# Node sums ahead of the transposes in TensorE's order of the first layer

## What is computed

```python
h = relu(layernorm(x))                                # 12500 x 16
hidden = relu(edge_attr_16 @ W1 + b1)                 # 412500 x 256
w_edge = (hidden @ W2 + b2).reshape(-1, 16, 16)       # a 16x16 matrix for each edge
msgs   = einsum('ei,eio->eo', h[src], w_edge)         # 412500 x 16
aggr   = segment_sum(msgs, dst)                       # 12500 x 16
x      = x + relu(batchnorm(aggr + h @ root + bias))
```

## Time and profile before

| | before |
|---|---|
| median of three runs | 8360.46 us (8337.11 to 8364.19) |
| the profiled execution | 8371.47 us, span 8369.5 us |
| mean granted TensorE clock | 0.941 |
| TensorE matmul busy | 7304.6 us, 87% |
| VectorE busy | 6439.7 us, 77% |
| GpSimd busy | 5810.0 us, 69% |
| ScalarE busy | 4454.8 us, 53% |
| first layer, first to last gather | 59.4 to 5086.6 us |

### The profile page before, as it was taken

The page is one execution under the profiler, slowest core; times in us unless marked ns, Lnnn a source line. Parts: engine busy times, 40 slices in busy tenths (PEclk is TensorE's granted clock), DMA queues, the critical chain, the costliest instruction groups (busy, mean ns, idle before and its releaser), DMA issues. The chain is left out here.

```text
span 8369.5 us, 188597 instructions
## 1 busy us (share of the span) xinstructions
PE 7304.6 (87%) x52097; PEld 6359.6 (76%) x52097; DVE 6439.7 (77%) x16833; ACT 4454.8 (53%) x8278; POOL 5810.0 (69%) x4953
## 2 busy tenths in 40 slices
PE   6888887888888888888888886999999999999998
PEld 5666666666666666666666664999999999999996
DVE  6666666666666666666666667999999999999997
ACT  3333333333333333333333334777878777777874
POOL 5666666666666666666666664888888888888886
PEclk8999999999999999999999998999999999999999
DMA  2000001000000000000000004444444455554444
GB/s 50 16 16 16 16 16 16 16 16 16 16 16 16 16 16 16 16 16 16 16 16 16 16 16 96 75 73 73 74 73 75 73 72 73 73 72 74 74 73 65
DMA packets 702593, 335.08 MB, mean 40 GB/s; under 512 B 423055, under 2 KB 646234, under 8 KB 702562
## 3 DMA queue, kind: packets, MB, share of 16 engines
q0 software_dynamic: 336128, 66.50, 12.9%
q1 hardware_dynamic: 365248, 264.73, 12.9%
q10 hardware_dynamic: 1186, 3.51, 0.1%
HBM read 301.49 MB, written 32.76 MB: 40 GB/s over the span
## 5 line engine op out<-in xcount | busy, mean ns | idle before, releaser
L728 POOL DMA_INDIRECT xg<-gather_rows,idx x3232 | 3144.1, 973 | 1905.1 <-issue 1874.3
L838 PE MATMUL ps_w<-W2s,hT 128*128 128x256 f32 x12928 | 3351.9, 416 | 148.6 <-issue 137.8
L838 PEld LDWEIGHTS ps_w<-W2s,hT 128*128 128x128 f32 x12928 | 2726.1, 211 | 762.3 <-issue 250.7
L1590 POOL DMA_INDIRECT sums<-total,row x1616 | 2570.5, 1591 | 539.1 <-issue 437.5
L1553 PE MATMUL ps_wide<-hot_col,placed 128*128 128x392 f32 x12928 | 2434.1, 345 | 11.6 <-issue 5.1
L1553 PEld LDWEIGHTS ps_wide<-hot_col,placed 128*128 128x128 f32 x12928 | 2313.1, 195 | 38.8 <-issue 22.9
L767 ACT ACTIVATE hT<-ps_h,b1c 128x512 f32<-128x512 f32 x1616 | 1023.0, 681 | 2442.1 <-PE ps_h L826 1954.0
L899 DVE TENSOR_TENSOR prod<-ps_w,xg 128x512 f32<-128x512 f32 x1616 | 1097.7, 690 | 1285.0 <-remote 985.9
L1389 DVE SCALAR_TENSOR_TENSOR placed<-ps_r,src_r,halves 128x512 fp32r<-128x512 f32 x1616 | 1096.8, 740 | 0.1
L1488 ACT ACTIVATE square<-iota_col,minus_col 128x784 bf16<-128x784 int16 x1212 | 1059.1, 936 | 60.9 <-issue 52.1
L906 DVE TENSOR_REDUCE msg<-prod 128x32 f32<-128x512 f32 x1616 | 1058.8, 676 | 0.0
(11 more groups left out here) (203 smaller groups left out, 4680.8 us busy)
## 6 DMA issues: line engine op xcount, KB each, us to landing
dst_row<-dst_rows SPq DMA_DIRECT2D x404, 256.0 KB
xg<-gather_rows,idx POOLq DMA_INDIRECT x3232
src_row<-src_rows SPq DMA_DIRECT2D x404, 128.0 KB
q_win<-q_rows SPq DMA_DIRECT2D x404, 96.0 KB
ea<-in_edge_attr SPq DMA_DIRECT2D x404, 64.0 KB
sums<-total,row POOLq DMA_INDIRECT x1616
e<-in_edge_attr SPq DMA_DIRECT2D x404, 32.0 KB
q_rows<-Q SPq DMA_DIRECT2D x12, 768.0 KB, 5.4
```

The costliest lines, as they stand in the source:

```text
L728: pool.indirect_dma_start(xg[r][:, t, :], None, k.rows, bass.IndirectOffsetOnAxis(ap=idx[r][:, t:t + 1], axis=0)).then_inc(xg_in[r][t], 16)
L838: last = pe.matmul(bank[:, w, :, :].rearrange("p i o -> p (i o)"), hT[half][:, j, col:col + P], k.W2[:, j, :], start=(j == 0), stop=(j == 1))
L1590: pool.indirect_dma_start(k.sums[t], bass.IndirectOffsetOnAxis(ap=row[r][:, t:t + 1], axis=0), total[r][:, t, :], None, compute_op=ALU.add ...
```

## The change

In body g of TensorE the two last blocks change places. The node sums of group g-1 stand ahead of the transposes of group g+2. Nothing else changes, on no engine.

```diff
                     edge_weights(g * 2 + 1, 1, (0, 1))
+                    if ahead or g >= 1:
+                        scatter(g - 1, 1 - s)
                     if ahead or g + 2 < G:
                         turn(g + 2)
-                    if ahead or g >= 1:
-                        scatter(g - 1, 1 - s)
                 each(pe, G, body, head=4, tail=2)
                 scatter(G - 1, 1)
```

## The result

| | median us | lowest to highest | runs |
|---|---|---|---|
| before | 8348.78 | 8322.31 to 8364.19 | 4 |
| after | 8439.15 | 8435.90 to 8441.74 | 4 |

The ratio is 1.0109, with a 95% interval from 1.0087 to 1.0132: the change costs 1.1%. The table has one run of before more than the prediction had; it was the quickest, so the median stands 12 us lower than the 8360.46 us from which the prediction started. The profiled execution of after took 8435.9 us, 64 us more than that of before (8371.5 us), which lay above its own median.

A forecast was written before the change was run, and what follows sets the result against it. A loop through GpSimd, restarted by TensorE's burst, was taken to set the pace. Terms 0 + 0 + 0 + 76 us gave 8448 us against the profiled execution, 8437 us (+0.9%) against the median; range 8345 to 8500 us.

The forecast's parts named there:

- a loop through GpSimd: First layer: eight gathers, the wait for TensorE's burst and the restart set the pace, 12.45 us a group, 5030 us.
- The signs named in the prediction: Profile after: restarts 12.6 us apart, GpSimd idle about 0.2 us more a group, 1.55 us to burst and TensorE busy time unchanged.
- (a): TensorE's work: the same instructions in another order, 0 us; any lost overlap between neighbours is covered by the stall.
- (b): Node sums finish earlier, but VectorE's L953 stands behind others of its own queue and gains nothing: 0 us.
- (c): The sums' wait for L923 and one-hot rows now precedes the transposes; 1.67 us to spare, so 0 us.
- (d): GpSimd's first gather waits for transposes told behind 16 sums: 0.19 us a group, 76 us; bounds 0 and 225 us.
- The equal shares: Burst of 0.295 us split evenly over 8 transposes, 16 sums and 1 hidden product, giving the sums 0.19 us.
- The sign of 0.83 us that becomes 1.0 us: Interval from VectorE's start on the last L838 product to GpSimd's restart should grow from 0.83 to 1.0 us.
- Rival 1: Pace set elsewhere, for instance by TensorE's 60 products per group, so the order changes nothing: 8360 us; chance 0.22.
- second road: Stall is TensorE waiting for its instructions at the loop's branch, equal in either order: 8360 us; within the 0.22.
- Rival 2: Later first gather leaves TensorE 0.19 us more to itself per group: 76 us less, 8284 us; chance 0.10.
- Rival 3: Stall catches TensorE inside the block, leaving transposes to issue: up to 0.56 us a group, 8585 us; chance 0.10.

The follow-up runs named there:

- gate_on_sums_2: Kernel before, with GpSimd's gathers waiting for the node sums behind the transposes instead of the transposes, on a chip with the stall: 8448.96 us, ratio 1.0102.
- swap_gate_on_sums: Kernel after, with gathers waiting for the node sums ahead of the transposes instead of the transposes, on the chip without the stall: 7372.88 us, ratio 1.0000 against before.
- no_gathers: Kernel before without any gathers from the fifth group on, old source rows used again, on a chip with the stall: 7075.4 us, ratio 0.8532.
- gate_on_weights_2: Kernel before, with gathers waiting for the edge weights ahead of the transposes instead of the transposes, on a chip with the stall: 8369.3 us, ratio 1.0013.
- no_gate: Kernel before without the gathers' wait for the transposes; they wait for indices and buffer only; chip with the stall: 9256.79 us, ratio 1.1161.
- swap_gate_2: Kernel after, with gathers waiting for the node sums ahead of the transposes, on a chip with the stall: 8416.37 us, ratio 1.0065 against before.
- gate_on_weights: Kernel before, with gathers waiting for the edge weights ahead of the transposes, on the chip without the stall: 7372.64 us, ratio 1.0000.

## Why the prediction was right, and where it was not

**The bound.** The step that carried the rest, a loop through GpSimd that TensorE's burst restarts, was right on the chips with the stall. Moving the signal alone gives the whole loss, leaving out a gather gives a whole gather, and leaving all out removes the stall. The gathers start a fixed 0.762 us behind the transposes' signal before and after. The signs named in the prediction came: restarts 12.55 to 12.62 us apart for 12.6, 0.19 us more idle per group for about 0.2, and 1.55 us to the burst that stay (medians 1.61 and 1.63 us). L761 still follows directly behind L767 (2420.38 + 1.26, and 2421.53). One did not: TensorE's busy time was to stay and grew by 42 us. `gate_on_sums_2` has the same growth, so it is a companion of the longer stall.

**(a) Work of TensorE and (b) earlier sums: 0 and 0.** Right as far as the runs reach. With the gate free of both blocks' place, on the chip without the stall, TensorE's new order is worth 0.0% (`swap_gate_on_sums`).

**(c) The wait that moves: 0 by cover.** Right. The sums show no idle time in after. In the group shown L923 ended at 2413.65 and the sums started at 2416.91. The line for L923, from the same timeline as above:

```profile
2413.37 0.28 DVE L923 TENSOR_TENSOR parts<-msg_res,parts 128x128 bf16<-128x128 f32 x1
```

The cover was 3.26 us there, more than the 1.67 us of the prediction.

**(d) The transposes told later: 0.19 us a group.** Right in kind, a little too large in size. The signals give 0.159 us for the 16 sums; times 401 that is 64 us, where the prediction had 76. The mean period grew by 0.17 us, 69 us over the layer, and the two profiled executions lie 64 us apart, the rest of the program having been 5 us shorter. The equal shares were the error: a sum takes 0.0099 us in the burst where a transpose takes 0.0116 us, and of the 0.295 us only 0.252 go to these 24 products. The sign of 0.83 us that becomes 1.0 us came, where like is compared with like. The burst tells the last two edge weights one after the other, and VectorE may begin with either. Where it begins with the last one, as in the prediction's row, the median is 0.83 us before and 0.99 us after (139 and 141 of the 402 groups); where it begins with the one before, it is 0.94 and 1.10 us (226 and 245 groups).

That 8437 us was forecast and 8439 us measured is in part luck. The fourth run of before put its median at 8348.8 us, so the change of the medians is 90 us and not 76. The profiled execution of before was 23 us above this median, which is most of what separates 64 from 90; the runs of before spread over 42 us, those of after over 6.

**Rival 1, nothing moves,** fell with `gate_on_sums_2`: TensorE's order untouched, 1.0% lost. Its second road, instructions that have to be fetched at the branch, fails already on the trace of before. Over the whole run it has 10 and 21 packets in its two instruction queues; the DMA queues of the stretch from 200 to 5000 us, with a stall in each group, are these two and no instruction queue:

```profile
q0 software_dynamic: 98702, 50.74, 7.9%
q1 hardware_dynamic: 55440, 25.26, 1.8%
```

`no_gathers`, where the branches stayed and the stall went, agrees. The Trainium skill (Runtime: NRT & Kernel Launch, "Instruction fetch mechanics") has the rule from which that road came; no run here shows a fetch that costs time. On one chip rival 1's outcome would hold for another reason: there GpSimd never waits for the gate. The change as it stands was not run on that chip; its order with the gate moved was, at 1.0000.

**Rival 2, faster,** fell: both measurements of the change show a loss, and the stall did not shorten.

**Rival 3, slower by more,** came half true, and the prediction did not see how often. The group shown above is such a case, with transposes left to issue at the burst. In the trace of after it is so in some 245 of the 402 groups counted. But it costs little: from the edge weights' signal to the transposes' the median is 0.25 us in groups with up to four left, 0.30 us with five and 0.33 us with seven, where the rival's price was 0.56 us. Over all groups, the distance from the sums' signal to the transposes' is 0.106 us in the mean and 0.093 us in the median; by this, what is left over costs 0.013 us a group, 5 us in all.

**The misses of the experiments** belong to the same reading. I took the loop for the only tie, so that each us off it would be a us gained. It holds upward, for delays. Downward it does not: with the gate earlier by 8 products the gain is taken back by the few groups whose signal comes ahead of the stall (`gate_on_weights_2`), and with the gate away the stall lands on other results and a longer loop closes (`no_gate`). `swap_gate_2` is not back at before because 16 sums are ahead of its signal where before has 8 transposes. The expectation had counted these and allowed 0.1 us a group, 40 us; the run lost 50. By the signals the place is worth 0.07 us a group and the moved gate 0.03 us; the last 10 us are not explained.

**What stays open.** What holds TensorE's completions and issues while GpSimd gathers, and whether it is the issue of the gathers or their transfers, no run tells. Nor does one tell why one chip doesn't show it, or whether this belongs to the chip at all: no two sets of experiments were run on the same chip, so chip and occasion are not told apart.

## What to carry to other kernels

Where a wait has no releaser in the profile and another engine's queue runs with a regular period, look at which signal restarts that queue, and treat that signal's place as part of the loop: eight small products more ahead of it were worth 0.6% here and sixteen 1%, though TensorE's work stayed the same. Test it by moving the wait alone to a neighbouring signal; this separates the order of the work from the moment it is told; and look at several groups, as one may begin with another signal than the next. And don't take away a pacing wait because it is idle time: its removal cost 11.6%, since what it paces then collides with work that more depends on.

## What the runs showed of the hardware

- **The same kernel takes 7373 us on one chip and 8297 to 8366 us on others**, with a spread of 0.1% among the 27 runs on the first. With the stall a group takes 12.45 us, without it 10.05 us, where the gathers run back to back (read in `gate_on_weights`, whose time is that of before there). A profile of one chip would have led to another bound than a profile of the other, and, as far as `swap_gate_on_sums` tells (1.0000 there, 1.0065 with the stall), to another answer on this change.
- **Gathers issued by GpSimd hold TensorE back on the chips with the stall.** TensorE runs densely beside the first six or seven of the eight gathers. Then its products start about 0.7 or 1.4 us apart (2418.98 behind 2418.23, and 2419.85 behind 2418.43), and their ends are told to the others only some 1.6 us after the last gather's end. Leaving the gathers out saves 3.1 us per group (1221 us over 400 groups), the gathers' own row included.
- **In the burst the ends of TensorE's products are told one after another**: 0.093 us for 8 transposes and 0.159 us for 16 sums, about 0.010 us each, where the 16 sums take 0.400 us without a stall. So the place of a signal in a burst counts, even when all of its work has long been issued.
- **TensorE's start times in the trace run ahead of what the others see.** In the earlier trace rows the edge weights start at 2411.56 and are busy for 3.62 us, and VectorE sees the last of them at 2419.76. An interval from a product's start to its consumer measures the stall, not the product.
